# Rotary sum on GpSimd, three buffers in place of four, one load semaphore fewer, and a different hand-written order of the attention

## The chip, the cores and the metric

The kernel runs on one core of a Trainium2 chip: TensorE (PE), VectorE (DVE), ScalarE (ACT), GpSimd (POOL) and SyncE (SP), which only issues DMAs here. The metric is the device time of one execution in microseconds. The kernel before took 2048.04 us in the median of three runs (2046.98 to 2052.48).

## The reference

Two layers on x of shape (2, 1024, 256), each an attention part and a feed-forward part, with a layer norm after each. The change touches the first attention alone:

```python
q = x @ Wq + bq; k = x @ Wk + bk; v = x @ Wv + bv      # 32 query heads, 8 key and value heads, D = 8
q = _rope(q.reshape(b, t, 32, 8).transpose(0, 2, 1, 3)); k = _rope(...)
q = q.reshape(b, 8, 4, t, 8)                            # 4 query heads share one key head
att = jnp.einsum('bkgid,bkjd->bkgij', q, k) / sqrt(8)
att = softmax(where(causal, att, -inf))
y = jnp.einsum('bkgij,bkjd->bkgid', att, v)
x = _layernorm(x + y @ Wo + bo)
x = _layernorm(x + ffn0(x)); x = _layernorm(x + gated_delta(x)); x = _layernorm(x + ffn1(x))
```

## The kernel before

**The projection** (`load_and_project`, the first 62 us). x is transposed on PE. Then ten jobs follow, two for K and eight for Q, each of 512 tokens: PE forms the product and its half-swapped twin in two PSUM banks, DVE multiplies one by the cosine table (L273) and the other by the sine table (L275) and adds the two (L280, the rotary sum `rot`). The fp32 result is stored as three bf16 parts: ACT rounds it (`high`, L239), DVE subtracts (`split`, L251), ACT rounds the rest (`middle`, L231), DVE subtracts again (`split_low`, L255). DVE takes the subtractions of jobs m-1 and m-2 in the iteration of job m. SP stores three parts per job to DRAM, and between them fetches the K rows (after job 5) and the Q rows (after job 7) of the first unit. `parts` has four buffers (`DEPTH`), `rot` and `rest` three (`RING`). All engines meet at a barrier when the phase ends.

**The attention** (`attention`, 62 to 465 us). A unit is one batch and one key head with its four query heads; there are 16. Per unit:
- 20 score tiles (`s1`, L537 and the causal mask L542): PE writes q k^T, DVE takes row maxima (L614). They use a ring of two tiles in PSUM. Tiles 0 and 8 have 512 elements per partition, 2, 3, 14 and 15 have 768, the others 1024.
- `nm` joins the maxima, `turn` transposes them on PE (L549), DVE copies them to SBUF (L625, `nmT`), POOL cuts them into three bf16 parts in five steps (`cut`, L510 to L518), SP writes them with six DMAs into the rows of q (`rows`, L453). I call this the row chain.
- 40 weight tiles (`st`, L558): PE recomputes k q^T with the maxima subtracted through those rows, ACT takes the exponential (L592) in a ring of three PSUM banks. Tile 0 waits for the first three rows' DMAs, tile 1 for the other three.
- POOL zeroes the masked corners (`hide`, L503). PE multiplies by v in 12 `pv` steps (L572). ACT copies the result out (`o`), SP stores it and loads the next unit's q and k (`qk`, twelve DMAs).
- Every fourth unit SP loads the denominators (`den`), DVE takes the reciprocal (`rec`, L435), SP stores and reloads it, POOL scales y (`scale`, L428).

Each engine walks its own list in the table `ATT_ORDER`, once per stage. A is the youngest unit in flight, E the oldest: on PE, `E.st.20` is weight tile 20 of unit n, `D.s1.19` score tile 19 of unit n+1, `C.s1.0` score tile 0 of unit n+2. An engine takes its list strictly in that order, so an instruction that waits holds up all behind it.

## Time and profile before

| | |
|---|---|
| median of three runs | 2048.04 us (2046.98 to 2052.48) |
| the profiled execution | 2048.04 us, span 2046.3 us |
| PE busy over the span | 1908.7 us (93%) |
| DVE busy | 1639.5 us (80%) |
| ACT busy | 1296.8 us (63%) |
| POOL busy | 722.4 us (35%) |
| projection, attention | 0 to 62 us, 62 to 465 us |

How to read the rows below. A timeline row gives the start in us, the length in us, the engine (SPq is SP's DMA queue, where the length is that of issuing), the source line, the operation, what it writes and reads with shapes, and how many merged instructions it holds; in brackets the idle time before it and what ended it. A row of windows gives a stretch and each engine's busy time in it with the number of instructions, PE first (then PE's weight loads, DVE, ACT, POOL), the granted TensorE clock (1.00 is 2.4 GHz), the share of the DMA engines and GB/s. A row of grouped instructions gives the count after x, then total busy us, mean ns of one, and the idle time before them. A row of one line's instructions gives min, median and max in ns.

### The profile page before, as it was taken

What the parts mean: (1) busy time and instruction counts of PE and PEld (TensorE: products, weight loads), DVE (VectorE), ACT (ScalarE), POOL (GpSimd) and SP (SyncE); (2) the same over time, 40 slices, a digit from 0 to 9 for tenths busy, and PEclk for the clock granted to TensorE, in tenths of its full rate; (3) what the DMA queues carried; (4) which work ended last, traced back from release to release, by engine and by line L of the source; (5) the groups of instructions that cost most, each with busy time, mean ns of one, the idle gap of its engine ahead of it and who ended that gap; (6) DMA issues with size and microseconds to landing.
All of it is one profiled execution on the core that took longest, in us unless ns stands there. A gap on an engine that the chain in (4) does not pass through costs nothing. (4 is left out here: it accounts for less than half of the span.)

```text
span 2046.3 us, 64605 instructions
## 1 busy us (share of the span) xinstructions
PE 1908.7 (93%) x27132; PEld 1439.8 (70%) x27132; DVE 1639.5 (80%) x3073; ACT 1296.8 (63%) x2818; POOL 722.4 (35%) x993
## 2 busy tenths in 40 slices
PE   8699999998985999999999999999999999999767
PEld 4233333326874788888888888888888888888656
DVE  6798999944655688888888888888888988888456
ACT  3188888894423476676666667667666666766553
POOL 1244444443231233243343333433433432432323
PEclk9599999999986999999999999999999999999979
DMA  5211121201001111111101101111011111010011
...
DMA packets 74191, 79.57 MB, mean 39 GB/s; under 512 B 13296, under 2 KB 60784, under 8 KB 73904
## 3 DMA queue, kind: packets, MB, share of 16 engines
...
q8 instruction: 217, 3.56, 0.7%
...
## 5 line engine op out<-in xcount | busy, mean ns | idle before, releaser
L1801 DVE SCALAR_TENSOR_TENSOR d_acc<-ps,d_par,d_acc 128x1023 f32<-128x1023 f32 (+2 forms) x288 | 363.8, 1263 | 16.6 <-ACT d_acc L1682 14.7
L1498 PE MATMUL ps<-x1p,d_wh 128*128 128x512 f32 x1024 | 357.6, 431 | 14.4 <-DVE d_acc L1801 9.6
L592 ACT ACTIVATE a_prob<-ps 128x512 f32<-128x512 f32 (+2 forms) x640 | 309.2, 562 | 91.0 <-PE ps L558 85.6
L614 DVE TENSOR_REDUCE a_mx<-ps 128x2 f32<-128x1024 f32 (+2 forms) x320 | 335.2, 1112 | 27.5 <-PE ps L542 21.3
L1682 ACT ACTIVATE d_acc<-ps,d_par 128x512 f32<-128x512 f32 x192 | 149.1, 776 | 142.4 <-PE ps L1498 138.2
L1432 POOL TENSOR_TENSOR d_og_l<-d_o_g,d_og_h 128x512 fp32r<-128x512 f32 x64 | 82.5, 1290 | 353.0 <-ACT d_og_h L1778 353.0
L1498 PE MATMUL ps<-x1p,d_wl 128*128 128x512 f32 x512 | 204.4, 399 | 0.0
L1498 PEld LDWEIGHTS ps<-x1p,d_wh 128*128 128x128 f32 x1024 | 172.6, 193 | 38.3 <-DVE d_acc L1801 10.8
L537 PE MATMUL ps<-k,q 48*128 48x512 bf16 (+3 forms) x768 | 155.9, 351 | 24.7 <-DVE a_mx L614 14.4
L558 PE MATMUL ps<-q,k 51*128 51x512 bf16 (+2 forms) x640 | 175.6, 365 | 1.8 <-ACT a_prob L592 0.9
L503 POOL TENSOR_SCALAR_AFFINE_SELECT a_prob<-a_prob 128x128 f32<-128x128 f32 (+1 forms) x384 | 126.0, 333 | 124.2 <-ACT a_prob L592 113.6
L572 PE MATMUL ps<-a_prob,a_v 128*32 128x512 f32 (+3 forms) x1536 | 165.0, 502 | 0.4 <-POOL a_prob L503 0.2
L1752 ACT ACTIVATE d_w_sb<-ps 128x128 f32<-128x128 f32 x256 | 70.9, 277 | 108.5 <-PE ps L1628 104.4
L558 PEld LDWEIGHTS ps<-q,k 51*128 51x128 bf16 x640 | 52.1, 94 | 110.0 <-ACT a_prob L592 92.7
L1526 PE MATMUL ps<-d_kq 128*128 128x256 f32 x512 | 126.8, 381 | 0.0
L1850 DVE SCALAR_TENSOR_TENSOR d_r_sb<-ps,d_ss,d_vtok 128x128 f32<-128x128 f32 x224 | 77.6, 347 | 58.0 <-PE ps L1610 58.0
L1875 DVE SCALAR_TENSOR_TENSOR d_o_g<-d_gate,d_o_g 128x512 f32<-128x512 f32 x64 | 110.9, 1732 | 4.9 <-ACT d_o_g L1771 4.9
L1498 PEld LDWEIGHTS ps<-x1p,d_wl 128*128 128x128 f32 x512 | 98.0, 191 | 22.7
L537 PEld LDWEIGHTS ps<-k,q 48*128 48x128 bf16 x768 | 43.3, 95 | 92.7 <-DVE a_mx L614 69.1
L1763 ACT ACTIVATE d_o_sb<-d_o_sb,d_nm,d_rs 128x128 f32<-128x128 f32 x256 | 102.3, 483 | 4.5 <-POOL d_nm L1464 3.7
L1610 PE MATMUL ps<-d_state,d_kq 128*128 128x128 f32 x448 | 96.5, 297 | 6.0 <-DVE d_state L1858 5.4
L1758 ACT ACTIVATE d_o_sb<-ps 128x128 f32<-128x128 f32 x256 | 69.4, 271 | 48.2 <-PE ps L1640 47.3
...
## 6 DMA issues: line engine op xcount, KB each, us to landing
d_abc<-scratch_alpha SPq DMA_DIRECT2D x32, 512.0 KB, 4.1
d_gb<-scratch_g SPq DMA_DIRECT2D x32, 512.0 KB, 3.8
d_wr<-in_dw SPq DMA_DIRECT2D x16, 512.0 KB, 5.2
...
x_tok<-in_x SPq DMA_DIRECT2D x4, 512.0 KB, 7.3
...
```

Of the source, the lines that this page charges most:

```text
L503: inc(nc.gpsimd.affine_select(w, w, [[0, heads], [1, P]], ALU.is_ge, zero, base=0, channel_multiplier=-1), "hide")
L537: last = nc.tensor.matmul(ps[:, bank + r, h * w:(h + 1) * w], q[p][s, h0 + h, i * P:(i + 1) * P], k[p][s, c0:c0 + w], start=True, stop=not ...
L558: inc(nc.tensor.matmul(ps[:, bank, 0:heads * (HALF - off)].rearrange("p (h c) -> p h c", c=HALF - off), k[p][s, j * P:(j + 1) * P], q[p][s ...
L572: last = nc.tensor.matmul(ps[g * VW:(g + 1) * VW, O, off:], v1[n % 2][:, j, :], prob[:, y % PB, g, off:], start=(j == 0), stop=(y + 1 in H ...
L592: inc(nc.scalar.activation(prob[:, y % PB, g:g + heads, off:], ps[:, PLACE["st", n, x], 0:heads * w].rearrange("p (h c) -> p h c", c=w), A ...
L614: inc(nc.vector.tensor_reduce(out, ps[:, bank:bank + 2, 0:heads * w].rearrange("p r (h c) -> p r h c", c=w), AX.X, ALU.max, negate=True), ...
L1498: last = nc.tensor.matmul(ps[:, bank, :], wp[g][:, k, i, :], x(part), start=(k == 0 and j == 0), stop=(k == KE - 1 and j == 2))
L1526: last = nc.tensor.matmul(ps[:, bank, 2 * i * P:2 * (i + 1) * P], kqc[:, 0, :], kqc.rearrange("p i t -> p (i t)"), start=True, stop=True)
L1682: inc(nc.scalar.activation(acc[i][:, h * HALF:(h + 1) * HALF], ps[:, PROJ + h, :], ACT.Identity, bias=par[p][:, 12 + i:13 + i], scale=par[ ...
L1763: ins = nc.scalar.activation(o_sb[n % 2][:, c, :], o_sb[n % 2][:, c, :], ACT.Identity, bias=nm[:, c:c + 1], scale=rs[:, c:c + 1])
L1801: inc(nc.vector.scalar_tensor_tensor(acc[i][:, d:T], taps[:, 0:T - d], par[p][:, 4 * i + j:4 * i + j + 1], acc[i][:, d:T], ALU.mult, ALU.a ...
L1875: inc(nc.vector.scalar_tensor_tensor(o_g[n % 2][:, c], gate[n % 2][:, c], 1.0, o_g[n % 2][:, c], ALU.add, ALU.mult), "gated")
```

## The change

Six edits:
1. The rotary sum moves from DVE to POOL, which does it for each job as soon as both products are there; DVE no longer waits for its own products.
2. `parts` has three buffers. ACT's rounding of job m waits for the stores of job m-3, not m-4.
3. The loads of the K bias and of both tables count on the same semaphore as the K weights; PE's first K job now waits for all five loads, as DVE's does.
4. The scratch for K in DRAM is laid out by head and then token over both batches, not by batch, head and token; store and fetch patterns follow.
5. On PE the score tiles and the `turn` come later among the weight tiles, the `pv` steps move by up to four weight tiles. DVE copies `nmT` after score tile 0 of the next unit, not after tile 2, and takes the reciprocal ahead of that copy, not behind it.
6. POOL's copy of v stands ahead of hide 32, not 38, and its scaling behind hide 31 of the same unit, not behind hide 3. ACT's and SP's orders are the same cycle, cut at another place.

Line numbers behind the new POOL code are four higher from the attention on (the turn is L549 before and L553 now).

```diff
@@ -87,8 +87,8 @@
-                src = dram["k"][part, n * D:(n + 1) * D, :]
-                sp.dma_start(cst["k"][p][s, :], bass.AP(src.tensor, src.offset, [[0, count], [T, D], [1, T]])).then_inc(arrived, 16)
+                src = dram["k"][part, kv * D:(kv + 1) * D, b * T:(b + 1) * T]
+                sp.dma_start(cst["k"][p][s, :], bass.AP(src.tensor, src.offset, [[0, count], [TOK, D], [1, T]])).then_inc(arrived, 16)
@@ -107,20 +107,20 @@
-        RING, DEPTH = 3, 4
+        RING = 3
-        parts = sb("p_parts", [P, DEPTH, 3, HALF], BF16)
+        parts = sb("p_parts", [P, RING, 3, HALF], BF16)
-        ident_in, k_in, tables_in, q_in, v_in = sem("p_ident_in"), sem("p_k_in"), sem("p_tables_in"), sem("p_q_in"), sem("p_v_in")
+        ident_in, k_in, q_in, v_in = sem("p_ident_in"), sem("p_k_in"), sem("p_q_in"), sem("p_v_in")
-        low, stored = sem("p_low"), [sem(f"p_stored{i}") for i in range(DEPTH)]
+        low, stored = sem("p_low"), [sem(f"p_stored{i}") for i in range(RING)]
@@ -136,9 +136,9 @@
-                sp.dma_start(bk[r * KR:(r + 1) * KR, :], w["bk"]).then_inc(tables_in, 16)
-            sp.dma_start(cos[:], w["cos"]).then_inc(tables_in, 16)
-            sp.dma_start(sin[:], w["sin"]).then_inc(tables_in, 16)
+                sp.dma_start(bk[r * KR:(r + 1) * KR, :], w["bk"]).then_inc(k_in, 16)
+            sp.dma_start(cos[:], w["cos"]).then_inc(k_in, 16)
+            sp.dma_start(sin[:], w["sin"]).then_inc(k_in, 16)
@@ -155,18 +155,19 @@
-                    sp.dma_start(dst, parts[:, m % DEPTH, s, :]).then_inc(stored[m % DEPTH], 16)
+                        dst = bass.AP(dst.tensor, dst.offset, [[T, B], [TOK, KR], [1, HALF]])
+                    sp.dma_start(dst, parts[:, m % RING, s, :]).then_inc(stored[m % RING], 16)
-                        sp.wait_ge(stored[o % DEPTH], 48 * (o // DEPTH + 1))
+                        sp.wait_ge(stored[o % RING], 48 * (o // RING + 1))
-                        sp.wait_ge(stored[o % DEPTH], 48 * (o // DEPTH + 1))
+                        sp.wait_ge(stored[o % RING], 48 * (o // RING + 1))
-            for s in range(DEPTH):
-                sp.wait_ge(stored[s], 48 * len(range(s, len(jobs), DEPTH)))
+            for s in range(RING):
+                sp.wait_ge(stored[s], 48 * len(range(s, len(jobs), RING)))
@@ -185,7 +186,7 @@
-                    pe.wait_ge(k_in, 16)
+                    pe.wait_ge(k_in, 16 * (3 + B))
@@ -218,6 +219,11 @@
+            for m in range(len(jobs)):
+                pool.wait_ge(rotated, 2 * m + 2)
+                if m >= RING:
+                    pool.wait_ge(high_left, m - RING + 1)
+                nc.gpsimd.tensor_tensor(rot[:, m % RING], t1[:, m % 2], t2[:, m % 2], ALU.add).then_inc(summed, 1)
@@ -228,15 +234,15 @@
-                nc.scalar.activation(parts[:, m % DEPTH, 1], rest[:, m % RING], ACT.Copy).then_inc(mid, 1)
+                nc.scalar.activation(parts[:, m % RING, 1], rest[:, m % RING], ACT.Copy).then_inc(mid, 1)
-                if m >= DEPTH:
-                    act.wait_ge(stored[m % DEPTH], 48 * (m // DEPTH))
-                nc.scalar.activation(parts[:, m % DEPTH, 0], rot[:, m % RING], ACT.Copy).then_inc(high, 1)
+                if m >= RING:
+                    act.wait_ge(stored[m % RING], 48 * (m // RING))
+                nc.scalar.activation(parts[:, m % RING, 0], rot[:, m % RING], ACT.Copy).then_inc(high, 1)
@@ -248,11 +254,11 @@
-                nc.vector.tensor_tensor(rest[:, m % RING], rot[:, m % RING], parts[:, m % DEPTH, 0], ALU.subtract).then_inc(high_left, 1)
+                nc.vector.tensor_tensor(rest[:, m % RING], rot[:, m % RING], parts[:, m % RING, 0], ALU.subtract).then_inc(high_left, 1)
-                nc.vector.tensor_tensor(parts[:, m % DEPTH, 2], rest[:, m % RING], parts[:, m % DEPTH, 1],
+                nc.vector.tensor_tensor(parts[:, m % RING, 2], rest[:, m % RING], parts[:, m % RING, 1],
@@ -263,7 +269,7 @@
-                    dve.wait_ge(tables_in, 16 * (2 + B))
+                    dve.wait_ge(k_in, 16 * (3 + B))
@@ -276,8 +282,6 @@
-                dve.wait_ge(rotated, 2 * m + 2)
-                nc.vector.tensor_tensor(rot[:, m % RING], t1[:, m % 2], t2[:, m % 2], ALU.add).then_inc(summed, 1)
@@ -306,20 +310,20 @@
 ATT_ORDER = {
-        E.st.10 D.s1.17 E.st.11 E.st.12 D.s1.18 E.st.13 E.st.14 E.pv.1 D.s1.19 E.st.15 E.st.16 E.pv.2 E.st.17 C.s1.0 E.st.18 C.s1.1 E.st.19 E.st.20
...
+        E.st.10 D.s1.13 E.st.11 E.st.12 D.s1.14 E.st.13 E.st.14 E.pv.1 D.s1.15 E.st.15 E.st.16 D.s1.16 E.st.17 E.pv.2 D.s1.17 E.st.18 E.st.19 E.pv.3
...
     "DVE": """
-        C.s1.16 C.s1.17 C.s1.18 C.s1.19 C.nm B.s1.0 B.s1.1 B.s1.2 C.turn E.rec B.s1.3 B.s1.4 B.s1.5 B.s1.6 B.s1.7 B.s1.8 B.s1.9 B.s1.10 B.s1.11
...
+        C.s1.1 C.s1.2 C.s1.3 C.s1.4 C.s1.5 C.s1.6 C.s1.7 C.s1.8 C.s1.9 C.s1.10 C.s1.11 C.s1.12 C.s1.13 C.s1.14 C.s1.15 C.s1.16 C.s1.17 C.s1.18
+        C.s1.19 C.nm B.s1.0 E.rec C.turn""",
...
@@ -2119,7 +2123,7 @@
-                   "k": nc.dram_tensor("scratch_k", [3, B * HKV * D, T], BF16).ap(),
+                   "k": nc.dram_tensor("scratch_k", [3, HKV * D, TOK], BF16).ap(),
```

PE, in the middle of the attention, around the transpose of the maxima (`ident,a_mx`). Before:

```order
L572 MATMUL ps<-a_prob,a_v 32x128 x4
L537 MATMUL ps<-k,q 128x384 x2
L542 MATMUL ps<-hidden,step 128x128 x2
L542 MATMUL ps<-hidden,step 128x64 x2
L558 MATMUL ps<-q,k 128x512 x2
L549 MATMUL ps<-ident,a_mx 32x128
L572 MATMUL ps<-a_prob,a_v 32x512 x4
L537 MATMUL ps<-k,q 128x384 x2
L542 MATMUL ps<-hidden,step 128x128 x2
L542 MATMUL ps<-hidden,step 128x64 x2
L558 MATMUL ps<-q,k 128x512
```

Now:

```order
L576 MATMUL ps<-a_prob,a_v 32x512 x4
L562 MATMUL ps<-q,k 128x512
L541 MATMUL ps<-k,q 128x128 x2
L546 MATMUL ps<-hidden,step 128x128 x2
L546 MATMUL ps<-hidden,step 128x64 x2
L541 MATMUL ps<-k,q 128x128 x2
L546 MATMUL ps<-hidden,step 128x128 x2
L546 MATMUL ps<-hidden,step 128x64 x2
L562 MATMUL ps<-q,k 128x512 x3
L553 MATMUL ps<-ident,a_mx 32x128
L541 MATMUL ps<-k,q 128x256 x2
L546 MATMUL ps<-hidden,step 128x128 x2
```

`k,q` rows with their `hidden,step` masks are score tiles (128x384 is tile 2 or 3, 128x128 tile 0, 128x256 tile 1), `q,k` rows are weight tiles, `a_prob,a_v` is a pv step. The turn stood behind two weight tiles and directly ahead of a pv step; now it stands behind three weight tiles, behind that pv step and behind score tile 0.

DVE, in the first unit that takes a reciprocal, from the last part of `nm` on. Before:

```order
L620 TENSOR_TENSOR a_mx<-a_mx 128x4x4
L614 TENSOR_REDUCE a_mx<-ps 128x4 x2
L614 TENSOR_REDUCE a_mx<-ps 128x2
L625 COPY a_nmT<-ps 32x128
L435 RECIPROCAL a_rec<-a_den 128x128
L614 TENSOR_REDUCE a_mx<-ps 128x2 x5
```

Now:

```order
L624 TENSOR_TENSOR a_mx<-a_mx 128x4x4
L618 TENSOR_REDUCE a_mx<-ps 128x4
L439 RECIPROCAL a_rec<-a_den 128x128
L629 COPY a_nmT<-ps 32x128
L618 TENSOR_REDUCE a_mx<-ps 128x4
L618 TENSOR_REDUCE a_mx<-ps 128x2 x6
```

`128x4` is a maximum over two heads' tiles, `128x2` over one. Two maxima less stand ahead of the copy, and the reciprocal stands ahead of it.

POOL, at the end of the projection. Before:

```order
L214 MEMSET pow_half 128x8
L215 MEMSET v_aug 128x4096
L217 MEMSET v_aug 128x128
L219 MEMSET k 128x1024 x4
L33 UNCONDITIONAL_BRANCH
L35 ISA
```

Now:

```order
L215 MEMSET pow_half 128x8
L216 MEMSET v_aug 128x4096
L218 MEMSET v_aug 128x128
L220 MEMSET k 128x1024 x4
L226 ISA
L226 TENSOR_TENSOR p_rot<-p_t 128x512 x10
L33 UNCONDITIONAL_BRANCH
L35 ISA
```

The ten sums come behind the memsets and ahead of the phase's barrier.

## Rows read from the trace of the kernel before

**Rows 1.** Windows, one stretch of the attention:

```profile
260.00:300.00 40.00, 38.05 (x431) 14.12 (x430) 36.20 (x39) 34.54 (x72) 16.33 (x50) 1.00 0.21 56
```

**Rows 2.** Timeline of DVE, the copy L625 and one reciprocal:

```profile
249.73 0.27 DVE L625 COPY a_nmT<-ps 32x128 f32<-32x128 f32 x1
...
272.41 0.27 DVE L625 COPY a_nmT<-ps 32x128 f32<-32x128 f32 x1
...
295.09 0.27 DVE L625 COPY a_nmT<-ps 32x128 f32<-32x128 f32 x1
297.70 0.95 DVE L435 RECIPROCAL a_rec<-a_den 128x128 f32<-128x128 f32 x1 [2.34 <-DMA a_den<-scratch_y]
...
319.52 0.27 DVE L625 COPY a_nmT<-ps 32x128 f32<-32x128 f32 x1
```

**Rows 3.** Timeline of DVE, four more copies; last, the reciprocals grouped (100 to 420):

```profile
86.81 0.27 DVE L625 COPY a_nmT<-ps 32x128 f32<-32x128 f32 x1
...
201.03 0.27 DVE L625 COPY a_nmT<-ps 32x128 f32<-32x128 f32 x1
...
227.06 0.27 DVE L625 COPY a_nmT<-ps 32x128 f32<-32x128 f32 x1
...
433.22 0.28 DVE L625 COPY a_nmT<-ps 32x128 f32<-32x128 f32 x1 [1.87 <-PE ps L549]
...
L435 DVE RECIPROCAL a_rec<-a_den 128x128 f32<-128x128 f32 x3 | 2.9, 953 | 6.4 <-DMA a_den<-scratch_y 6.4
```

**Rows 4.** Timeline of the projection; second row, the sine table's issue to landing:

```profile
6.22 0.43 SPq L141 DMA_DIRECT2D p_sin<-in_c_sin  x1
p_sin<-in_c_sin SPq DMA_DIRECT2D x1, 512.0 KB, 6.9
...
12.03 7.09 PE L202 MATMUL ps<-yT,p_wk 128*64 128x512 f32 x32 [0.83 <-ACT yT L227]
...
41.87 0.69 DVE L280 TENSOR_TENSOR p_rot<-p_t 128x512 f32<-128x512 f32 x1
...
43.38 0.75 DVE L273 SCALAR_TENSOR_TENSOR p_t<-ps,p_bq,p_cos 128x512 f32<-128x512 f32 x1 [0.22 <-PE ps L197]
...
46.82 0.75 DVE L273 SCALAR_TENSOR_TENSOR p_t<-ps,p_bq,p_cos 128x512 f32<-128x512 f32 x1 [0.22 <-PE ps L197]
...
55.43 3.75 SPq L158 DMA_DIRECT2D scratch_q<-p_parts  x6
```

**Rows 5.** POOL's L1432 grouped; DVE's L1875 by line; both engines' timeline near 908:

```profile
L1432 POOL TENSOR_TENSOR d_og_l<-d_o_g,d_og_h 128x512 fp32r<-128x512 f32 x64 | 82.5, 1290 | 353.0 <-ACT d_og_h L1778 353.0
...
L1875 DVE SCALAR_TENSOR_TENSOR d_o_g<-d_gate,d_o_g x64: 650/1785/2872, 750.8 to 1939.6; 128x512 f32<-128x512 f32 x64
...
907.58 2.35 POOL L782 TENSOR_TENSOR d_wl<-d_wr,d_wh 128x1024 fp32r<-128x1024 f32 x1
...
908.70 1.78 DVE L1875 SCALAR_TENSOR_TENSOR d_o_g<-d_gate,d_o_g 128x512 f32<-128x512 f32 x1
```

**Rows 6.** Timeline of DVE and POOL after the last copy:

```profile
433.42 2.34 DVE L631 CAST g_wu<-g_raw_up 128x2048 fp32r<-128x2048 int8 x2
...
433.56 2.35 POOL L510 CAST a_nparts<-a_nmT 32x128 bf16<-32x128 f32 x1 [4.43 <-DVE a_nmT L625]
```

**Rows 7.** Grouped by shape, 100 to 420 us:

```profile
L614 DVE TENSOR_REDUCE a_mx<-ps 128x2 f32<-128x1024 f32 x165 | 193.9, 1219 | 8.1 <-PE ps L537 5.0 <-PE ps L542 3.0
...
L592 ACT ACTIVATE a_prob<-ps 128x512 f32<-128x512 f32 x388 | 208.0, 606 | 29.4 <-PE ps L558 28.0
```

**Rows 8.** The row chain: POOL's last step, SP's rows, issue to landing in us:

```profile
251.75 0.28 POOL L518 CAST a_nparts<-a_nrest 32x128 bf16<-32x128 f32 x1
252.06 3.73 SPq L453 DMA_DIRECT2D q<-a_nparts  x6
...
DMA to landing us min/median/max: 1.7/1.8/4.1
```

**Rows 9.** Timeline of ACT, where the last unit's weight tiles begin:

```profile
442.53 3.98 ACT L592 ACTIVATE a_prob<-ps 128x256 f32<-128x256 f32 x9 [0.32 <-PE ps L558]
```

More of the change, by code:

```diff
@@ L308 @@
     "PE": """
-        E.st.10 D.s1.17 E.st.11 E.st.12 D.s1.18 E.st.13 E.st.14 E.pv.1 D.s1.19 E.st.15 E.st.16 E.pv.2 E.st.17 C.s1.0 E.st.18 C.s1.1 E.st.19 E.st.20
-        E.pv.3 C.s1.2 E.st.21 E.st.22 D.turn E.pv.4 C.s1.3 E.st.23 C.s1.4 E.st.24 E.st.25 E.pv.5 E.st.26 C.s1.5 E.st.27 E.st.28 E.pv.6 C.s1.6
-        E.st.29 E.st.30 C.s1.7 E.st.31 E.pv.7 E.st.32 C.s1.8 E.st.33 E.st.34 C.s1.9 E.st.35 E.st.36 C.s1.10 E.st.37 E.pv.8 E.st.38 C.s1.11 E.st.39
-        D.st.0 D.st.1 C.s1.12 D.st.2 E.pv.9 D.st.3 C.s1.13 D.st.4 E.pv.10 D.st.5 C.s1.14 D.st.6 E.pv.11 D.st.7 C.s1.15 D.st.8 D.st.9 C.s1.16 D.pv.0""",
+        E.st.10 D.s1.13 E.st.11 E.st.12 D.s1.14 E.st.13 E.st.14 E.pv.1 D.s1.15 E.st.15 E.st.16 D.s1.16 E.st.17 E.pv.2 D.s1.17 E.st.18 E.st.19 E.pv.3
@@ L313 @@
+        E.st.20 D.s1.18 E.st.21 E.st.22 D.s1.19 E.pv.4 E.st.23 C.s1.0 E.st.24 E.st.25 E.st.26 D.turn C.s1.1 E.st.27 C.s1.2 E.st.28 E.st.29 E.pv.5
+        C.s1.3 E.st.30 E.st.31 E.st.32 C.s1.4 E.pv.6 E.st.33 E.st.34 C.s1.5 E.st.35 E.pv.7 E.st.36 E.st.37 C.s1.6 E.st.38 E.pv.8 E.st.39 C.s1.7
+        D.st.0 C.s1.8 D.st.1 D.st.2 E.pv.9 C.s1.9 D.st.3 D.st.4 E.pv.10 C.s1.10 D.st.5 D.st.6 E.pv.11 C.s1.11 D.st.7 D.st.8 D.st.9 C.s1.12 D.pv.0""",
     "ACT": """
-        E.st.20 E.st.21 E.st.22 E.st.23 E.st.24 E.st.25 E.st.26 E.st.27 E.st.28 E.st.29 E.st.30 E.st.31 E.st.32 E.st.33 E.st.34 E.st.35 E.st.36
@@ L315 @@
-        E.st.37 E.st.38 E.st.39 D.st.0 D.st.1 D.st.2 D.st.3 D.st.4 D.st.5 D.st.6 E.o.1 D.st.7 D.st.8 D.st.9 D.st.10 D.st.11 D.st.12 D.st.13 D.st.14
-        D.st.15 D.st.16 D.st.17 D.st.18 D.st.19 D.o.0""",
+        E.st.22 E.st.23 E.st.24 E.st.25 E.st.26 E.st.27 E.st.28 E.st.29 E.st.30 E.st.31 E.st.32 E.st.33 E.st.34 E.st.35 E.st.36 E.st.37 E.st.38
+        E.st.39 D.st.0 D.st.1 D.st.2 D.st.3 D.st.4 D.st.5 D.st.6 E.o.1 D.st.7 D.st.8 D.st.9 D.st.10 D.st.11 D.st.12 D.st.13 D.st.14 D.st.15 D.st.16
@@ L317 @@
+        D.st.17 D.st.18 D.st.19 D.o.0 D.st.20 D.st.21""",
     "DVE": """
-        C.s1.16 C.s1.17 C.s1.18 C.s1.19 C.nm B.s1.0 B.s1.1 B.s1.2 C.turn E.rec B.s1.3 B.s1.4 B.s1.5 B.s1.6 B.s1.7 B.s1.8 B.s1.9 B.s1.10 B.s1.11
-        B.s1.12 B.s1.13 B.s1.14 B.s1.15""",
+        C.s1.1 C.s1.2 C.s1.3 C.s1.4 C.s1.5 C.s1.6 C.s1.7 C.s1.8 C.s1.9 C.s1.10 C.s1.11 C.s1.12 C.s1.13 C.s1.14 C.s1.15 C.s1.16 C.s1.17 C.s1.18
+        C.s1.19 C.nm B.s1.0 E.rec C.turn""",
     "POOL": """
-        C.hide.34 C.hide.35 C.hide.36 C.hide.37 B.v C.hide.38 C.hide.39 B.hide.0 B.hide.1 B.hide.2 B.hide.3 E.scale B.hide.4 B.hide.5 B.hide.6
@@ L322 @@
-        B.hide.7 B.hide.8 B.hide.9 B.hide.10 B.hide.11 A.cut B.hide.28 B.hide.29 B.hide.30 B.hide.31 B.hide.32 B.hide.33""",
+        B.hide.5 B.hide.6 B.hide.7 B.hide.8 B.hide.9 B.hide.10 B.hide.11 A.cut B.hide.28 B.hide.29 B.hide.30 B.hide.31 A.v E.scale B.hide.32
+        B.hide.33 B.hide.34 B.hide.35 B.hide.36 B.hide.37 B.hide.38 B.hide.39 A.hide.0 A.hide.1 A.hide.2 A.hide.3 A.hide.4""",
     "SP": """
```

## The prediction

> **What bounds the kernel now.** I read first the busy shares, then the busy time by stretch, then DVE's timeline, then PE, ACT and POOL around one place of it.
> The change touches the projection (the first 62 us) and the attention (62 to 465 us); later stages run the same instructions, so I carry their time over. By stretch, PE, DVE and ACT are busy for 38, 36 and 35 of 40 us in the attention at full clock [rows 1]: three engines, coupled by rings of two score tiles and three weight tiles, and none has much to give. DVE's timeline shows the rhythm. The copy of the transposed maxima (once per unit) recurs every 22.68 us (249.73 to 272.41, again to 295.09) [rows 2]. In three of the sixteen units a reciprocal follows the copy and waits for its DMA: 295.09 to 319.52 is 24.43, 201.03 to 227.06 is 26.03 [rows 2, 3], 1.75 and 3.35 over a plain unit. All three together wait 6.4 us and work 2.9 [rows 3]; the third waits least and costs 0.9 over a plain unit, so 6.0 for the three. First to last copy, 86.81 to 433.22, is 346.4 us [rows 3].
>
> **The projection.** Three edits act there.
> (a) PE now also waits for the sine table. It is issued at 6.22 and lands 6.9 us later, at 13.1, where the first K matmul started at 12.03 [rows 4]. PE is busy from there on, job by job, so its whole row of jobs moves by 1.1 us.
> (b) The add of the two rotated halves leaves DVE. That frees one 0.69 us instruction per job, so the last part of a job is ready about 0.6 us earlier inside its iteration [rows 4]. POOL takes the add over; the nearest row is a POOL add of the same shape, 1.29 us [rows 5]. What ends the phase is SP's queue: from the stores of job 5 on it issues without a pause, with the six K fetches and six Q fetches between, and its last six stores start at 55.43 and take 3.75 us to issue [rows 4]. So only the time of job 5's last part counts: +1.1 - 0.6 = +0.5 us at best.
> (c) At worst POOL's add and DVE's subtractions get in each other's way. A DVE instruction with both inputs in SBUF takes 0.65 us alone, but 1.79 in the median; at 908.70 it took 1.78 and ended at 910.48, 0.55 us after POOL's subtraction of 907.58 was over (909.93): it had waited for POOL [rows 5]. DVE's two subtractions per job are of that kind. If POOL's add gets in between them, DVE's iteration is 0.67 + 0.66 + 0.60 for the rotation and the first subtraction (start to start), 1.29 for the block and 0.65 for the second, 3.87 against the 3.44 that PE takes for a job (43.38 to 46.82) [rows 4]. The 0.43 more is paid in the five jobs from 2 to 7, and the last part of job 5 is also 1.4 later in its iteration (1.29 for the block, and a little to start POOL): 1.1 - 0.6 + 2.2 + 1.4 = +4.1 us. If the subtractions run back to back, +0.5. In the one place where POOL waited beside two DVE casts in a row it lost to both: its cast started at 433.56 and took 2.35 us instead of 0.28, DVE's casts ended at 435.76 [rows 6]. No row shows two subtractions in a row with POOL waiting, so I take the middle, **+2.3** (0.5 to 4.1).
> The Trainium skill states that rule (SBUF — State Buffer, Who interferes with whom): a VectorE instruction with two SBUF inputs contends with a GpSimd instruction that reads SBUF, and whichever issues first holds the shared ports for its whole length. The trace agrees for POOL first (0.65 against 1.78 us) and, with a cast in place of the subtraction, for DVE first (0.28 against 2.35). In the projection DVE issues its first subtraction ahead of POOL's add and its second while POOL already waits; the rule does not say who has the ports then. With POOL it would give rival 3, 2049.4, with DVE 2045.8.
> (d) The ring of three parts in place of four makes ACT wait for the stores of job m-3. The worst is the last job, whose ACT copy must wait for job 6's stores, issued after the K fetches, so until about 53.2. From there high, subtraction, mid, subtraction are four instructions of 0.63 to 0.69, so the last part is ready near 56; SP wants it at about 57.9. Hidden, **0**; if SP were not late, it would cost up to 3. The new layout of K in DRAM keeps every run of 1 KB in the stores and 2 KB in the fetches: 0.
>
> **The attention, start.** PE and DVE work alone on score tiles here, DVE without a gap. In the new order the turn comes after score tile 0 of the next unit, not after tile 2, and DVE's copy likewise. Two maxima (one of 1.22 us, one of 0.95, less their overlap, and the 0.2 of wait in front of them) leave the stretch in front of the first copy: 86.81 becomes 84.6, **-2.2**. The reciprocals, period and end below are counted from copy to copy.
>
> **The period.** Each score tile is issued six to nine weight tiles later (tile 19 after weight tile 22, was 14), the turn four later (after 26, was 22). I walked both orders by hand, tile by tile. A maximum is 1.22 us long and an exponential 0.61 [rows 7], a next one starts 0.08 to 0.12 before the last ends; on PE a weight tile of 512 columns is 0.21 and a pv step of 512 is 1.0. A score tile needs the maximum of two tiles before, a weight tile the exponential of three before. Longest new waits: between pv steps 4 and 5 PE has weight tiles 24, 25, 26 in a row, and 26 waits for the exponential of 23, which was issued only after pv step 4; then the turn, a barrier of its own (it was directly ahead of a pv step); then 29, waiting for 26. From pv step 4's end to pv step 5's start this is 2.9 us, for 1.1 in the old order, while the stretches from pv 7 to pv 9 fall from 3.5 to 1.7, because score tiles 8 to 10 no longer queue up behind the maxima there. Summed over the twelve pv steps the old order gives 22.5 in this walk (read: 22.68), the new 22.7. So I take +0.2 per unit; bounds: -0.45 (28 groups of weight tiles between other work become 26, each a 0.21 us slot) and +0.5 (three in a row fill their ring of three, twice more per unit). Thirteen plain periods: **+2.6** (-5.9 to +6.5). The last period had no score tiles 0 to 2 in front of its copy; now it lacks only tile 0: 22.04 becomes 22.7, **+0.65**.
>
> **The reciprocals.** The DMA of the denominators is queued behind twelve loads on SP and lands at 297.6, unchanged relative to ACT. DVE stood at 295.36 and waited 2.34 [rows 2]. In the new order DVE comes there after score tile 0, which PE issues only after pv step 4 and weight tile 23; in the walk that is at about 297.1: wait 0.5, then 0.95 of work, and the turn's copy queues behind it, with the score tile after that. I take 1.0 us each, 3 against 6.0: **-3.0** (-4.5 to 0). The first of the old ones also contained a lower clock after PE's wait.
>
> **The row chain.** What the later turn uses up is slack. From the copy's start (249.73), POOL's five steps end at 252.03, SP starts six row DMAs at 252.06, 0.63 apart, each landing 1.7 to 1.8 after issue [rows 8]: the third at 255.1, the sixth at 256.95. So weight tile 0 may start 5.4 and tile 1 7.2 us after the copy. Old order: due at +10.0 and +10.3. New: thirteen weight tiles, seven score tiles and four pv steps lie between the turn and tile 0, and tile 1 is due at about +8.1 by the walk. Slack 0.9, so **0** in plain units. POOL's 2.4 us scaling, moved to behind hide 31, ends before pv step 9 wants hide 35: 0. In the last unit POOL's cast is the slow one (2.35) [rows 6] and the chain is 2.1 longer, 9.3 to tile 1, whose exponential then comes at +9.7; it came at 443.65, +10.4 (weight tile 38's exponential started at 442.53, two of 0.3 and one of 0.5 follow) [rows 9]. The end is thus not shortened by the four tiles but by **-0.75** (-0.75 to +1).
>
> **Sum.** 2.3 - 2.2 + 2.6 + 0.65 - 3.0 - 0.75 = -0.4. The profiled execution took 2048.04 us (span 2046.3), which is also the median of the three runs. Forecast **2047.6 us**.
>
> **Rivals.**
> 1. The row chain becomes the bound. Place: weight tile 1 of each unit. If landing takes 0.9 us more than read, or PE reaches the tile 0.9 earlier, each further 0.1 us is paid in 15 units. For: SP's rows stand behind the reciprocal's store and load in three units. Against: slack of 0.9 by the walk. At 0.6 per unit +9: 2056.6, slower.
> 2. The order is simply better balanced: a period of 22.2, for the DVE work of 21.3 has room for it and there are two slots less. -0.45 instead of +0.2 in 13 periods, and projection at its low end: 2047.6 - 8.5 - 1.8 = 2037.3. For: longer unbroken alternation of score and weight tiles. Against: the turn as a barrier of its own.
> 3. POOL wins every time in the projection: +1.8, 2049.4, and the row chain and period as forecast. For: 1.78 us read. Against: the casts.
> 4. The reciprocal's wait only moves, because the copy now stands behind it: +3.0, 2050.6.
>
> **Chances.** Forecast 0.50, rival 1 0.15, rival 2 0.11, rival 3 0.18, rival 4 0.06. No change means within 0.3% (6.1 us), which is about what runs of this kernel can tell. The forecast, 3 and 4 lie inside it. Faster 0.11, same 0.72, slower 0.17 (two hundredths for rivals 3 and 4 together with a period at +0.5). Range 2041.5 to 2054.5: without rivals 1 and 2 it holds nearly all.
>
> **What would show it.** Right: first K matmul near 13.2; the attention's first score tile near 64; first copy at 84.6 plus the projection's term; copies 22.8 to 23.0 apart; reciprocals waiting under 1 us; the last copy to the end of the exponentials about 30 us. Wrong: weight tiles waiting for the row DMA in plain units (rival 1), copies under 22.5 apart (rival 2), DVE's subtractions in the projection at 1.9 us (rival 3).

## The result, and the profile after

The changed kernel took 2058.64 us in the median of seven timed runs (2056.13 to 2065.9) against 2046.98 us before (2044.3 to 2052.48): ratio 1.0064, 95% interval 1.0048 to 1.008. It is slower, by 11.7 us, and outside my range of 2041.5 to 2054.5. (The ratios here and below are taken over all runs of a kernel, not from two medians, so the two can differ by a few us.) Its profiled execution is one of the longer ones, 2066.26 us, span 2064.5; four of its twelve executions, this among them, lie between 2064.8 and 2066.3, the other eight between 2056.1 and 2059.6.

The first thing to do with two profiles of such a kernel is to cut both at the same events: DVE's first maximum, the first copy, the last copy, the end of the attention's output copies, a table load behind the next stage. From the first maximum to the first copy I call the fill, from the last copy to the last output copy the last unit. Busy time by stretch, before (columns: stretch, its length, busy us and instructions of PE, PEld, DVE, ACT and POOL, PE's granted clock, share of the DMA engines, GB/s):

```profile
0.00:62.70 62.70, 48.16 (x207) 27.89 (x209) 36.73 (x58) 16.03 (x25) 8.23 (x12) 0.95 0.59 173
62.70:86.80 24.10, 15.51 (x131) 6.15 (x127) 23.64 (x24) 0.00 (x0) 8.17 (x1) 0.50 0.25 74
86.80:433.20 346.40, 334.81 (x3628) 122.15 (x3632) 318.57 (x331) 291.64 (x610) 150.93 (x441) 0.97 0.16 39
433.20:465.70 32.50, 29.81 (x217) 7.35 (x217) 2.55 (x3) 29.62 (x64) 17.06 (x44) 1.00 0.04 6
```

and after:

```profile
0.00:75.50 75.50, 51.82 (x208) 29.15 (x210) 36.67 (x49) 16.16 (x25) 23.70 (x22) 0.90 0.49 144
75.50:97.20 21.70, 14.00 (x113) 5.24 (x109) 21.50 (x22) 0.00 (x0) 8.01 (x1) 0.50 0.28 82
97.20:444.80 347.60, 334.83 (x3655) 119.91 (x3655) 322.95 (x333) 296.02 (x615) 145.84 (x440) 0.97 0.16 39
444.80:483.00 38.20, 34.67 (x205) 6.90 (x204) 2.55 (x3) 27.37 (x58) 18.64 (x45) 0.73 0.03 5
```

Projection +12.7 us (first maximum at 75.46, was 62.74), fill -2.3, copy to copy +1.2, last unit +5.8 (from the copy at 444.82 to the last output copy at 482.44 it is 37.62, was 31.84), all later stages +0.8: together the 18.2 between the two spans. Two of these are not in my sum.

The first is in SP's queue (start, time to issue, line, what, how many):

```profile
27.89 10.83 SPq L159 DMA_DIRECT2D scratch_k<-p_parts  x6
40.55 17.14 SPq L159 DMA_DIRECT2D scratch_q<-p_parts  x12
57.82 3.72 SPq L91 DMA_DIRECT2D k<-scratch_k  x6
61.58 3.83 SPq L159 DMA_DIRECT2D scratch_q<-p_parts  x6
65.51 2.49 SPq L88 DMA_DIRECT2D q<-scratch_q  x6
68.05 3.76 SPq L159 DMA_DIRECT2D scratch_q<-p_parts  x6
```

and the same K stores before:

```profile
26.08 4.67 SPq L158 DMA_DIRECT2D scratch_k<-p_parts  x6
```

Six K stores take 10.83 us to issue, 4.67 before. The last six Q stores start at 68.05, 12.6 later than in [rows 4]. ACT and DVE show who waits for them:

```profile
38.56 0.63 ACT L245 ACTIVATE p_parts<-p_rot 128x512 bf16<-128x512 f32 x1 [8.11 <-DMA scratch_k<-p_parts]
46.70 0.63 ACT L245 ACTIVATE p_parts<-p_rot 128x512 bf16<-128x512 f32 x1 [6.13 <-DMA scratch_k<-p_parts]
```

```profile
28.45 0.73 DVE L281 SCALAR_TENSOR_TENSOR p_t<-ps,p_bq,p_sin 128x512 f32<-128x512 f32 x1
29.11 0.68 DVE L257 TENSOR_TENSOR p_rest<-p_rot,p_parts 128x512 f32<-128x512 f32 x1
29.71 1.75 DVE L261 TENSOR_TENSOR p_parts<-p_rest,p_parts 128x512 bf16<-128x512 f32 x1
31.39 0.74 DVE L279 SCALAR_TENSOR_TENSOR p_t<-ps,p_bq,p_cos 128x512 f32<-128x512 f32 x1
39.22 0.69 DVE L257 TENSOR_TENSOR p_rest<-p_rot,p_parts 128x512 f32<-128x512 f32 x1 [6.44 <-ACT p_parts L245]
```

ACT's rounding of jobs 3 and 4 waits 14.2 us for the stores of jobs 0 and 1, DVE waits for ACT (14.0 us in three waits), and PE for DVE (5.8 us in two). The same rows answer the question that I had left between rivals: DVE's second subtraction (L261) is 1.75 us long, not 0.68. POOL's add (29.27, 1.65 us) gets in between the two.

The second is in the last unit. PE waits there for two row DMAs, and the granted clock falls to half (waits first, then windows with the columns of above):

```profile
452.23 0.39 PE L562 MATMUL ps<-q,k 51*128 51x512 bf16 x1 [0.36 <-DMA q<-a_nparts]
454.13 0.61 PE L562 MATMUL ps<-q,k 51*128 51x512 bf16 x2 [1.51 <-DMA q<-a_nparts]
```

```profile
449.00:453.00 4.00, 3.26 (x22) 0.61 (x21) 0.00 (x0) 3.11 (x8) 4.00 (x8) 1.00 0.04 5
453.00:457.00 4.00, 2.87 (x16) 0.61 (x20) 0.00 (x0) 1.59 (x4) 3.09 (x11) 0.58 0.01 1
457.00:461.00 4.00, 4.00 (x29) 0.77 (x21) 0.00 (x0) 3.45 (x8) 1.89 (x7) 0.50 0.09 13
461.00:467.00 6.00, 5.95 (x30) 0.96 (x26) 0.00 (x0) 3.74 (x8) 1.15 (x3) 0.50 0.09 16
```

In the middle of the attention the copies are evenly spaced, as forecast, and the reciprocals hardly wait:

```profile
237.58 0.28 DVE L629 COPY a_nmT<-ps 32x128 f32<-32x128 f32 x1
260.34 0.28 DVE L629 COPY a_nmT<-ps 32x128 f32<-32x128 f32 x1
283.10 0.28 DVE L629 COPY a_nmT<-ps 32x128 f32<-32x128 f32 x1
306.05 0.95 DVE L439 RECIPROCAL a_rec<-a_den 128x128 f32<-128x128 f32 x1 [0.28 <-DMA a_den<-scratch_y]
306.92 0.21 DVE L629 COPY a_nmT<-ps 32x128 f32<-32x128 f32 x1
```

The period is 22.76 us (22.68 in [rows 2]); all three reciprocals together wait 1.8 us (6.4 in [rows 3]).

### The profile page after: what moved, and what is told of

Same layout as the page of the kernel before. It is cut to its first block and busy times, and to the rows that moved or that the text cites. A ratio compares the mean times of both kernels' runs of the same rounds, so it can differ in the third digit from the quotient of the medians.

```text
span 2064.5 us, 64614 instructions
## 1 busy us (share of the span) xinstructions
PE 1918.4 (93%) x27132; PEld 1440.4 (70%) x27132; DVE 1640.1 (79%) x3063; ACT 1297.5 (63%) x2818; POOL 733.9 (36%) x1003
## 5 line engine op out<-in xcount | busy, mean ns | idle before, releaser
L576 PE MATMUL ps<-a_prob,a_v 128*32 128x512 f32 (+3 forms) x1536 | 170.4, 518 | 0.0
L562 PE MATMUL ps<-q,k 51*128 51x512 bf16 (+2 forms) x640 | 162.6, 372 | 7.3 <-ACT a_prob L596 3.4
L541 PE MATMUL ps<-k,q 48*128 48x512 bf16 (+3 forms) x768 | 142.8, 348 | 25.8 <-DVE a_mx L618 12.4
L562 PEld LDWEIGHTS ps<-q,k 51*128 51x128 bf16 x640 | 45.5, 94 | 112.2 <-ACT a_prob L596 100.1
```

Of the source, the lines that this page charges most:

```text
L541: last = nc.tensor.matmul(ps[:, bank + r, h * w:(h + 1) * w], q[p][s, h0 + h, i * P:(i + 1) * P], k[p][s, c0:c0 + w], start=True, stop=not ...
L562: inc(nc.tensor.matmul(ps[:, bank, 0:heads * (HALF - off)].rearrange("p (h c) -> p h c", c=HALF - off), k[p][s, j * P:(j + 1) * P], q[p][s ...
L576: last = nc.tensor.matmul(ps[g * VW:(g + 1) * VW, O, off:], v1[n % 2][:, j, :], prob[:, y % PB, g, off:], start=(j == 0), stop=(y + 1 in H ...
```

## The experiments

**Theories.** A: the new K store, a DMA of 2 x 64 x 512, is carried by two of the 16 DMA engines. B: the ring of three parts alone makes ACT wait. C: rows 4 KB apart in DRAM are slow to write. F: any store of three dimensions is slow, whatever its outermost count. For the end, D: PE's wait for the last unit's rows makes the clock fall, and that is what makes some runs longer. E: the spread comes from the projection. G: the clock falls for the new order itself.

Runs of before, on the chip of each group, had medians of 2048.46, 2048.98, 2047.06 and 2047.86 us; each result below is compared with those of its own group.

**1. The K stores in two parts each.** From the changed kernel (the waits for the stores count the doubled number, not shown):

```diff
-    dst = bass.AP(dst.tensor, dst.offset, [[T, B], [TOK, KR], [1, HALF]])
-    sp.dma_start(dst, parts[:, m % RING, s, :])
+    for b in range(B):
+        sp.dma_start(dram["k"][s, :, b * T + n * HALF:b * T + (n + 1) * HALF], parts[b * KR:(b + 1) * KR, m % RING, s, :])
```

> The changed kernel, with each K store written as two DMAs (one for each batch, 64 partitions x 512, rows still 4 KB apart in DRAM) instead of one DMA of 2 x 64 x 512. Ring of three, POOL's add and the new order stay. Theory A (a DMA whose outermost dimension is 2 is carried by two of the 16 DMA engines): landings of the K stores fall from 5 to 11 us to about 2, ACT no longer waits 8.1 and 6.1 us for them, the attention starts near 65 instead of 75.5: 2048 to 2050 us in place of 2058.6. Theory B (the ring of three alone makes ACT wait): no change, 2057 to 2060. Theory C (rows 4 KB apart in DRAM are slow to write): no change either, 2057 to 2060, with long landings.

2051.53 us (11 runs, 2049.05 to 2055.46), ratio 1.0018 (1.001 to 1.0027). First maximum at 66.88. The stores, still with rows 4 KB apart, land in 1.9 to 2.1 us. B and C fall. The median is 1.5 us over the 2048 to 2050 that I expected. Part of it is twelve K stores in SP's queue in place of six: they take 7.52 us to issue, 2.6 more than six of 128 x 512 in the same kernel (4.89, experiment 12), and the first maximum comes 1.5 later than there (65.38).

**2. Four parts again, K stores as changed.** From the changed kernel:

```diff
-    parts = sb("p_parts", [P, RING, 3, HALF], BF16)
+    parts = sb("p_parts", [P, 4, 3, HALF], BF16)       # and m % 4 wherever parts and stored are indexed
```

> The changed kernel with the ring of parts back at four; the K stores stay one DMA of 2 x 64 x 512. Theory A and C (slow K stores): the job that waits for them is one later: ACT waits for job 0's stores at job 4, until about 38.5, and for job 1's at job 5, until about 46.5, so one job of 3.5 us is gained: about 2055, first score tile near 72. Theory B (ring of three): the waits go, first score tile near 64, 2047.

2054.61 us, ratio 1.0032 (1.002 to 1.0044), first maximum at 71.78. As A and C expected: one job is gained, the slow stores stay.

**3. The order alone.** Before with the new table:

```diff
-    E.st.10 D.s1.17 E.st.11 E.st.12 D.s1.18 ...
+    E.st.10 D.s1.13 E.st.11 E.st.12 D.s1.14 ...
```

> The kernel before with the new order of the attention alone; the projection is that of before. From the trace of the changed kernel: first copy 2.3 us earlier after the same start (near 84.5), copies 347.6 us first to last in place of 346.4. If the last unit's two waits for its row DMAs leave TensorE at full clock, its end is 0 to 0.7 shorter: 2045 us. If TensorE falls to half clock behind them, as in the profile of the changed kernel, the end is 5.8 longer: 2052. Theory D (that fall is what makes some runs 7 us longer than the others): both values are found among the runs of this kernel. Theory E (the spread of the changed kernel comes from its projection): all runs within 2 us of 2045.

2047.91 us (2045.3 to 2053.98), ratio 1.0005 (0.9993 to 1.0017). Seven of twelve runs lie at 2045.3 to 2048.4, five at 2052.2 to 2054.0, as D expected; E falls. (The kernel before spreads as well in this group, from 2045.1 to 2052.1, but without a gap.) The profile, one of the five, has the first copy at 84.48 and 347.1 us to the last. PE has the same two waits for the rows as in the changed kernel, and half the clock behind them:

```profile
438.00:442.00 4.00, 2.12 (x16) 0.44 (x12) 0.00 (x0) 2.33 (x6) 4.00 (x9) 1.00 0.03 4
442.00:446.00 4.00, 4.00 (x31) 1.06 (x31) 0.00 (x0) 3.52 (x9) 2.33 (x9) 0.54 0.00 0
446.00:452.00 6.00, 5.95 (x32) 0.85 (x24) 0.00 (x0) 3.81 (x10) 1.58 (x4) 0.50 0.15 25
```

But the clock is back near 453, and the last unit is 34.27 us, only 3.0 over the 31.2 of the profiles in which it came back soon. The stages behind the attention are 4.6 us longer than in the profile of before (1585.8 for 1581.2), so the last unit explains less than half of this long run.

**4. The K layout alone.** From the kernel before:

```diff
+    dst = bass.AP(dst.tensor, dst.offset, [[T, B], [TOK, KR], [1, HALF]])
-    "k": nc.dram_tensor("scratch_k", [3, B * HKV * D, T], BF16)
+    "k": nc.dram_tensor("scratch_k", [3, HKV * D, TOK], BF16)      # the fetch likewise
```

> The kernel before with the new K layout alone (one DMA of 2 x 64 x 512 per store, rows 4 KB apart; ring of four, DVE's add, old order). Theory A and C: K stores land late, ACT waits at jobs 4 and 5 until about 36.5 and 45, the first score tile comes 6 to 9 us later than 62.7: 2053 to 2056. Theory B (ring of three is the cause): no change, 2047.

2056.48 us (five runs), ratio 1.0043 (1.0029 to 1.0057), first maximum at 70.06. So layout alone makes it slower, with four parts too.

**5 to 7. The form of the store at nearly the same addresses.** K in DRAM by batch as before, rows 2 KB apart, and one spare row behind every 64, 32 or 8 (here 64), so that the store has the form 2 x 64, 4 x 32 or 16 x 8 rows of 512:

```diff
-    "k": nc.dram_tensor("scratch_k", [3, B * HKV * D, T], BF16)
+    "k": nc.dram_tensor("scratch_k", [3, 2, 64 + 1, T], BF16)
-    dst = dram["k"][s, :, cols]
+    dst = dram["k"][s, :, 0:64, cols]
-    src = dram["k"][part, n * D:(n + 1) * D, :]
+    src = dram["k"][part, n * D // 64, n * D % 64:n * D % 64 + D, :]
```

> The kernel before, K kept by batch as before (rows 2 KB apart) but with one spare row in DRAM behind every 64, so that a K store is a DMA of 2 x 64 x 512 and not of 128 x 512. Ring of four, nothing else changed. Theory A (two DMA engines carry it): the six K stores take 10.8 us to issue as with the new layout, DMA moves 48 GB/s while they run, the attention starts 7 us later: 2054 to 2057. Theory C (rows 4 KB apart): landings of 1.8 us as before, 2047 to 2048.

> The same with a spare row behind every 32 rows: a K store of 4 x 32 x 512. Theory A: four DMA engines, 96 GB/s while they run, a store of 128 KB lands after about 1.4 us of moving plus the fixed part, so 3 to 4 us; three stores of a job are through in 4.1 us, just more than a job's 3.44, so nearly nothing waits: attention start within 1 us of 62.7, 2047 to 2049. Theory C: as before.

> The same with a spare row behind every 8 rows: a K store of 16 x 8 x 512. Theory A: 16 engines as before, landing 1.7 to 2.4 us, attention start 62.7. A rival F (any store of three dimensions is slow, whatever the outermost count) expects it as late as with 2 x 64 x 512.

With 2 x 64 x 512: 2057.43 us, ratio 1.0034 (1.0023 to 1.0046), first maximum 70.99. With 4 x 32 x 512: one run, 2048.01, 62.93. With 16 x 8 x 512: one run, 2049.04, 62.66. In the 4 x 32 kernel ACT still waits 1.8 us for K stores (10.6 with 2 x 64, none with 16 x 8). While K stores run, the windows (same columns as above) show for the three, each from its own kernel:

```profile
30.00:37.00 7.00, 7.00 (x18) 3.06 (x17) 4.70 (x8) 0.78 (x2) 0.00 (x0) 1.00 0.14 48
```

```profile
29.00:33.00 4.00, 4.00 (x10) 1.71 (x9) 3.78 (x7) 1.31 (x3) 0.00 (x0) 1.00 0.27 88
```

```profile
26.50:29.00 2.50, 2.50 (x7) 1.07 (x6) 2.50 (x5) 0.88 (x2) 0.00 (x0) 1.00 0.54 144
```

The DMA share is the busy share of 16 engines: 0.14 x 16 is 2.2 engines, 0.27 x 16 is 4.3, 0.54 x 16 is 8.6. In the changed kernel, from 31 to 38 us, it is 0.13 at 47 GB/s. The share is a mean and names no engine, but for 2 and for 4 it stays flat at what two and four busy engines make (0.125 and 0.25), and that is A. The rate for 4 is 88 GB/s, not quite the 96 that I expected. With two engines I estimate 131 kB / 48 GB/s = 2.7 us for a store of 128 KB and 8.2 for the three of a job; with the 2 us that a plain store takes to land, the two jobs that are issued from 27.89 land at about 38 and 46, where ACT's waits end (38.56 and 46.70). C and F fall.

**8. The casts behind the cut** (before with the new order, and one wait more on DVE, at the end of the attention):

```diff
+    W("low", UNITS - 1, 1)
     dve.wait_ge(w.arrived, w.count)
     for u in range(w.n_up):
         nc.vector.tensor_copy(w.wu[:, u], w.up[:, u])
```

> The kernel before with the new order, and DVE's two casts of the next stage's weights at the end of the attention wait until POOL's cut of the last unit is through. Theory D (what makes some runs 7 us longer is the wait of TensorE for the last unit's row DMAs, which are 2.1 us late because POOL's first cast takes 2.35 us beside DVE's, and the fall to half clock behind it): POOL's cast takes 0.28, the row DMAs are issued 2.3 us after the copy, TensorE waits less than 0.5 us for them and stays at full clock, and all runs lie at 2044 to 2047. Theory G (the clock falls for the new order itself, without a wait): the long runs near 2053 stay.

2045.48 us (2043.72 to 2054.34), ratio 0.9989 (0.9977 to 1.0001). POOL's first cast of the last unit falls from 2.35 us to 0.28:

```profile
430.22 0.28 POOL L510 CAST a_nparts<-a_nmT 32x128 bf16<-32x128 f32 x1 [7.99 <-DVE a_nmT L625]
431.90 0.28 POOL L518 CAST a_nparts<-a_nrest 32x128 bf16<-32x128 f32 x1
432.15 3.05 POOL L503 TENSOR_SCALAR_AFFINE_SELECT a_prob<-a_prob 128x128 f32<-128x128 f32 x4
```

One of twelve runs is above 2050 (2054.34), where it was five of twelve in experiment 3, on another chip; chance alone would make a split at least as uneven about one time in thirteen. But the last row shows a price: DVE's casts now lie beside POOL's masks (3.05 us for four, 1.04 in experiment 3), a `pv` step waits 1.2 us for a mask, and the clock still falls, for some 4 us (0.57 from 439 to 443). The last unit is 32.11 us. This agrees with D and doesn't prove it: the wait has moved and become shorter, and not all runs lie at the expected 2044 to 2047.

**9 to 11. The projection's other edits, one by one,** each alone on before.

```diff
9:  - dve:  nc.vector.tensor_tensor(rot[:, m % RING], t1[:, m % 2], t2[:, m % 2], ALU.add)
    + pool: nc.gpsimd.tensor_tensor(rot[:, m % RING], t1[:, m % 2], t2[:, m % 2], ALU.add)
10: - pe.wait_ge(k_in, 16)
    + pe.wait_ge(k_in, 16 * (3 + B))
11: - RING, DEPTH = 3, 4
    + RING, DEPTH = 3, 3
```

> The kernel before with the add of the rotated halves on POOL alone (all waits, layout, ring and order of before). If POOL takes the ports between DVE's two subtractions each time (as in the profile of the changed kernel): DVE's second subtraction 1.75 us, POOL's add 1.65, DVE's iteration 3.60, which is 0.16 over TensorE's 3.44, and the last part of each job 1 us later: SP's last stores start 0.5 to 1.5 us later than 55.4, the attention starts at 63.2 to 64.2: 2048 to 2050. If DVE keeps them: 0.6 earlier, 2047.

> The kernel before with TensorE's wait for the tables alone (one semaphore for the K weights, the biases and both tables). From rows: the sine table lands at 13.1 and the first K matmul started at 12.03, so the whole row of jobs moves by 1.1 to 1.4 us and the attention starts at 63.9 to 64.1: 2049. If that start is hidden by SP's queue, which ends the phase: 2048.

> The kernel before with a ring of three parts in place of four, K stores of 128 x 512 as before. ACT's high of job 3 waits for job 0's stores, which land 2 us after issue: these are out long before. The later jobs wait for stores of three jobs before, which SP issues in 0.6 us each: in the changed kernel ACT waited 1.1 us in each of three jobs for scratch_q stores. If that wait is covered: 2048. If it is paid in the jobs 5 to 9: up to 3 us, 2051. The 10 us of the changed kernel are not seen here (theory A).

POOL's add: 2048.41, ratio 1.0006 (0.9994 to 1.0018). Tables: 2048.91, 1.0011 (1.0002 to 1.0021). Ring of three: 2047.08, 1.0001 (0.9992 to 1.0011). The medians move by less than 2 us, and the loads at the kernel's start vary by nearly 1 us from profile to profile, so I measure from the first K store's issue to the attention's first maximum:

| kernel | first K store | first maximum | between |
|---|---|---|---|
| before | 26.08 | 62.74 | 36.66 |
| ring of three alone (11) | 26.98 | 63.75 | 36.77 |
| tables alone (10) | 27.33 | 64.03 | 36.70 |
| POOL's add alone (9) | 26.54 | 64.07 | 37.53 |
| K layout alone (4) | 25.99 | 70.06 | 44.07 |
| changed, old K layout (12) | 27.77 | 65.38 | 37.61 |
| changed, four parts (2) | 27.80 | 71.78 | 43.98 |
| changed | 27.89 | 75.46 | 47.57 |

Ring alone +0.1, POOL's add +0.9, layout alone +7.4; in the changed kernel the layout makes 47.57 - 37.61 = 10.0, so the ring of three, worth nothing by itself, costs a job once the stores are slow (47.57 - 43.98 = 3.6). The tables' 1.2 lie ahead of this stretch: in experiment 10 the first K matmul starts at 13.28, released by the sine table, and in the changed kernel at 13.37, for 12.03 before.

**12. The changed kernel with only the K layout undone.**

```diff
-    dst = bass.AP(dst.tensor, dst.offset, [[T, B], [TOK, KR], [1, HALF]])
-    "k": nc.dram_tensor("scratch_k", [3, HKV * D, TOK], BF16)
+    "k": nc.dram_tensor("scratch_k", [3, B * HKV * D, T], BF16)      # the fetch likewise
```

> The changed kernel with the K layout alone undone: K stores of 128 x 512 again, ring of three, POOL's add, the merged wait and the new order stay. Theory A: the attention starts 9 to 11 us earlier than 75.46, near 65 to 66 (62.7 + 1.3 for the tables + 1 for POOL's add + 0 to 1), and the time is that of the new order plus this: 2047 to 2050, with some runs 7 us longer if theory D holds. If other parts of the projection carry more than 3 us, 2052 or more.

2048.79 us (2046.11 to 2051.98), ratio 1.0005 (0.9996 to 1.0014), first maximum at 65.38. This is the changed kernel as I had it in mind: +0.9 us for a forecast of -0.4. D expected some runs 7 us longer; four of the eleven lie at 2050.4 to 2052.0, but that is only some 4 us over the others (2046.1 to 2049.0).

**13. The rows of the last unit late, in the old order** (before; SP waits for POOL's mask 31 of the unit before):

```diff
     W("low", n, 1)
+    if n == UNITS - 1:
+        W("hide", n - 1, MASKED.index(31) + 1)
```

> The kernel before, old order, in which SP issues the last unit's six row DMAs about 2.2 us later than it could (it also waits for POOL's mask 31 of the unit before). Theory D (a wait of TensorE for these rows makes the clock fall, and this is what the long runs are): TensorE waits 2 to 3 us in the last unit in the old order too, the profile or a share of the runs shows half clock behind it, and some runs are 5 to 8 us over the others: median 2049 to 2054. Theory G (it is the new order as such): every run 1 to 2.5 us longer, 2049, none near 2055.

2051.75 us (2048.53 to 2054.64), ratio 1.0018 (1.0007 to 1.0028). From the last copy to the last output copy 37.70 us, for 31.84 before and 37.62 in the changed kernel. Waits and windows of the last unit:

```profile
PEld ps L560 <- DMA q<-a_nparts: 2.4, 2, 1.8
PE ps L560 <- DMA q<-a_nparts: 1.5, 1, 1.5
```

```profile
438.00:442.00 4.00, 2.08 (x14) 0.45 (x13) 0.00 (x0) 2.47 (x6) 2.68 (x8) 0.86 0.05 6
442.00:446.00 4.00, 4.00 (x29) 0.81 (x28) 0.00 (x0) 2.19 (x5) 1.17 (x4) 0.50 0.00 0
446.00:452.00 6.00, 5.95 (x32) 0.99 (x24) 0.00 (x0) 4.76 (x11) 2.45 (x7) 0.50 0.15 25
```

PE is busy for 2.08 of 4 us, then has half the clock for some 12 us. It is the same picture in the old order, so the new order as such is not needed: G falls. For the last unit D is shown: late rows make PE wait, half clock follows, and wait and clock together cost 5.9 us. That this is what makes the longer runs is shown in part only. In the changed kernel's profile it is nearly the whole distance to the shorter runs (37.62 for 31.2), in experiment 3's less than half. The mean granted clock that is recorded for every execution is lower in the long runs of the changed kernel (0.953 to 0.956, the other eight 0.958 to 0.960), but a mean doesn't say in which stage it fell.

**14 and 15. The casts behind the cut, in the changed kernel and in the one before** (the one line of experiment 8 in each).

> The changed kernel with DVE's two casts behind the last unit's cut, nothing else. Theory D: the runs near 2065 (4 of 12 of the changed kernel) go nearly all, the others stay: 2057 to 2058 in the median, none or one of the runs over 2062. Theory G: a third of the runs stays near 2065.

2059.05 us (five runs, 2056.14 to 2061.9), ratio 1.0055 (1.0042 to 1.0068); none near 2065, last unit 31.97 us. As D expected (none or one over 2062; the median is 1 over its 2057 to 2058), though five runs could miss a share of one in three by chance (about one time in eight).

> The kernel before, old order, with DVE's two casts at the end of the attention behind POOL's cut of the last unit: the control for the new order with the same edit (2045.5). In the old order TensorE waited only 0.6 us in the last unit for its row DMAs, so taking these 2.1 us earlier is worth 0 to 0.6: 2047.5 to 2048.5. If the gain of 3 us was that of the casts and not of the order, this one shows 2045.5 too.

2047.96 us, ratio 1.0005 (0.9996 to 1.0014). So the edit by itself brings nothing in the old order, where PE waited 0.6 us for the rows.

## Why the prediction was wrong, step by step

- **The step that failed** is the last sentence of the projection: "The new layout of K in DRAM keeps every run of 1 KB in the stores and 2 KB in the fetches: 0." I had looked at the length of the runs and not at the shape of the pattern. Its cost is 10.1 us of the 12.7 in the projection (75.46 against 65.38), and nearly all of the 11.7 between the medians (0.9 without it): experiments 1, 4, 5 and 12 each show it from another side. The source of before wrote the store as `dram["k"][s, :, cols]`, 128 rows at one stride; the diff turned that into `[[T, B], [TOK, KR], [1, HALF]]`, with 2 outermost. The Trainium skill (DMA: Bandwidth & Descriptors, Why a DMA increments its semaphore by 16 and not by 1) has the rule: the number of engines is the largest up to 16 that divides the outermost count on both sides. The runs agree for 2 (share 0.13 to 0.14) and 4 (0.27); with 16 the share is 0.54, as with the plain store of before from 27 to 29 us, so it is no less spread than that one.
- **(d), ring of three: 0** "if SP were not late, it would cost up to 3". Alone 0.1, right. With the slow stores it costs 3.6 (experiment 2). I had priced the two edits apart, and their cost is not a sum: the ring decides how early a slow landing is felt.
- **(a) and (b, c), tables and POOL's add: +2.3** (0.5 to 4.1). Measured 2.64 (65.38 against 62.74, of which the loads at the start can vary by nearly 1); +1.2 and +0.9 one by one. But by another way than in the sum. POOL wins every time (rival 3 was right on that; the casts of [rows 6] were the wrong pattern), yet an iteration of DVE is 3.60 us and not 3.87, since the next rotation starts 0.07 before the long subtraction ends and this one is 1.75, not 1.94 (1.29 for the block and 0.65). The part over PE's 3.44 is thus 0.16 and not 0.43. The Trainium skill's rule (SBUF — State Buffer, Who interferes with whom), that the first to issue holds the ports for its whole length, agrees with a DVE instruction of 1.75 behind POOL.
- **Fill: -2.2.** 21.77 against 24.07: -2.3.
- **Period: +0.2 per unit.** +0.08, so 1.0 in thirteen and not 2.6. The forecast said 22.8 to 23.0 apart; 22.76.
- **Reciprocals: -3.0.** The waits are what I said, under 1 us each (1.8 in all, so the wait did not just move, as rival 4 had it), but their price is not 1.0 each. The copies from 189.28 to 237.58, 283.10 to 329.75 and 375.27 to 422.06 are two periods each and lie 2.8, 1.1 and 1.3 us over plain ones (the first again with half clock, 215 to 217): 5.2 for 6.0, a gain of 0.8 that is nearer to rival 4's 0 than to my 3.0. I read it so: 0.95 of work and 0.6 of wait are paid in full each time, which makes 4.7 of the 5.2, where I had set 1.0; no experiment isolates it. This term is off by 2.2, and the period makes up 1.6 of it: from first to last copy 347.6, for 346.4. Over all profiles of this study ten in the old order average 345.1 and seven in the new 347.1, so these terms together are +2.0 where my sum had +0.25; single profiles scatter widely (342.8 to 347.5, and 345.4 to 349.0).
- **Last unit: -0.75.** In the profiles in which PE got its clock back soon it is 31.2 (experiments 1, 2 and 12), so -0.6: right. But the slack that I called used up was below nothing: PE waited 1.9 us (first 0.36, then 1.51) for the rows, as the walk could have told (tile 1 at +9.3 after a due time of +8.1), and I priced the wait at nothing more than itself. With the half clock behind the wait the last unit is 5.8 longer than before in the profile shown, and 2.4 longer in that of experiment 3. A bound of +1 for this term was too narrow; what a stall of PE cost in clock stood in the rows of before, which I had used for the reciprocal alone.
- **Row chain, rival 1: false.** In all units but the last, loads for weight tiles wait for rows only 0.6 us, in two waits; in experiment 3's profile there is one of 1.5. **Rival 2: false**, the copies are 22.76 apart and not 22.2.
- **The sum.** Without the layout the forecast was 0.4 us less than before, and experiment 12 measured 0.9 more (ratio 1.0005); with it, 10 us are missing. That the rest comes so close is in part luck: the gain of the reciprocals was forecast 2.2 too large and the cost of the period 1.6 too large, and they nearly cancel. The range was built from terms that I had bounded; the one that I called 0 had no bound.

The best version found is number 8, the new order on the old projection with the casts behind the cut: 0.9989 of before (0.9977 to 1.0001), by the two ratios some 15 us under the changed kernel (1.0064). It is not shown to beat the kernel before, its interval ends at 1.0001.

**Still open:** why in experiments 1, 2 and 12 the clock falls for some 4 us ahead of the wait for the rows (0.50 from 440 to 442 in experiment 1), and is back afterwards, while in others it falls behind that wait and for longer; whether each of the longer runs has such a fall, since only profiled executions show their clock by stretch; and what makes the later stages of experiment 3's profile 4.6 us longer. I also did not try the new order with a turn some tiles earlier.
